# A counter raised by every matmul, and the biases loaded first, in an eight-core attention and FFN layer

## The chip, the cores and the metric

The kernel runs on one Trainium2 chip with all 8 cores. Each core computes 2 of the 16 sequences, with its own copy of the weights; the cores exchange nothing. The time is device microseconds of the slowest core. A core's engines are TensorE (PE in the profile, with its weight loads as PEld), VectorE (DVE), ScalarE (ACT), GpSimd (POOL) and SyncE (SP). Each works through its own list of instructions in order, and they wait for one another by counters (semaphores).

## The reference

`x` has the shape 16 x 4096 x 1024 in f32. There are 16 heads of 64; windows are 256 rows long and advance by 128, and within a window attention is over the 64 x 64 channel pairs of a head, not over rows:

```python
qkv = (x @ W_qkv + b_qkv)                      # 1024 -> 3072
attn = einsum('bhndw,bhnew->bhnde', qw, kw) * 64 ** -0.5
attn = softmax(attn, axis=-1)
o = einsum('bhnde,bhnew->bhndw', attn, vw)     # (b, h, n*d, w) reshaped
x = layernorm(x + o[:, :L] @ W_out + b_out)
gate, up = x @ wg.T, x @ wu.T                  # 1024 -> 3072, int32 weights / 127
x = layernorm(x + (silu(gate) * up) @ wd.T)
```

Since only the first 4096 rows of `o` are kept, 16 windows of each sequence count, made from 17 blocks of 128 rows.

## The kernel before

The program is written by hand, instruction by instruction, engine by engine, inside three blocks. A block ends and the next begins with a barrier of all five engines. Program order is the order in which `build_program` emits, and each instruction that another engine waits for raises a counter by `b.inc`; `b.wait` puts a wait ahead of the next instruction of an engine, unless the engine has waited for that value already. TensorE, VectorE, ScalarE and GpSimd have a counter each ("T", "V", "A", "G"); DMAs have counters of their own and raise them by 16.

The first block (L162 to L220) is the start. POOL clears some tiles and issues 18 DMAs that convert to bf16 on the way: in turns a chunk of 128 rows of `wqkv` (L178) and of `wout` (L180), eight of each, then the biases `bq_bf` and `bo_bf` (L182, L183). All raise "wi0". VectorE waits for all of them and scales the biases by 1/128 (L190, L191). Four rounds spread them over 128 partitions: TensorE multiplies a row of ones with 1024 of the bias elements into PSUM in two matmuls (L206, L207), VectorE copies the result (L214), and the next round waits for that copy. SP waits for the 18 DMAs and the last copy, and so keeps the block open.

The second block is attention and first layernorm, 32 windows on each core. For each block of 128 rows TensorE transposes x (L287), makes q, k and v in three passes (L528 and L533 for the two halves of 1024 columns, 8 chunks each, and L536 and L540 for the bias), and transposes v (L639). For each window it makes the scores of 16 heads in 32 matmuls of 64 columns (L593), transposes the softmax result A in 16 (L671, L673), multiplies it with v in 64 matmuls of 64 columns (L702), and makes the output projection for two blocks of rows (L738, L743, L747, L750). The two heads of a pair write to partitions 0 to 63 and 64 to 127 of PSUM. VectorE copies results out of PSUM, computes the softmax without its exponent and adds the residual; ScalarE evacuates L702's result into `attn_out` (L792), computes the exponent and the layernorm. TensorE also transposes y for the FFN (L322). Between these, the FFN weights are prepared, two jobs per window: POOL loads int32 rows as bf16, VectorE scales them (L403), TensorE transposes them (L417), VectorE copies (L429), POOL writes them to HBM (L439, L442).

The third block is the FFN for 32 groups of 256 rows, with 24 steps each: 8 gate matmuls (L1057) and 8 up matmuls (L1069) of 256 columns, silu on ScalarE (L1156), the product on VectorE (L1092), and 4 down matmuls of 512 columns for the step before (L1036, L1040). The second layernorm runs on ScalarE beside it.

In each group of matmuls one, the last, raises "T", for instance in the gate group:

```python
if dc == 7:
    b.inc(mm, "T", 1)
```

Exceptions are the bias matmuls L206, L207, L536, L540, L747 and L750, each of which raises it. Of the four down matmuls only the last, an L1040, does.

## Time and profile before

| | us |
|---|---|
| three timed runs | 3376.67, 3383.41, 3852.67 |
| their median | 3383.41 |
| profiled execution | 3376.9 |
| its span, slowest core (core 3) | 3375.3 |
| span of the fastest core | 3361.5 |
| PE busy on core 3 | 2936.9 (x23572 matmuls) |
| ACT, DVE, POOL busy | 1247.8, 935.1, 182.9 |

The span is from the first to the last instruction of a core in the profiled execution. Matmuls overlap in the array, and their ends are modelled, so that pace is read from starts: of two neighbours, or of the first and last of a group. A group in the timeline (x8) has one start and the time from there to its last end. "[1.35 <-DVE w_in_bf L403]" behind a row is idle time of that engine before it, and who ended it.

### The profile page before, as it was taken

The numbers are of one execution on the slowest core, as the hardware profiler recorded it, in microseconds if no ns is written. First come the engines' busy times: TensorE is split into PE (matmuls) and PEld (weight loads), VectorE is DVE, ScalarE is ACT, GpSimd is POOL, SyncE is SP. The second block draws the span as 40 slices with busy tenths as digits, with TensorE's granted clock in tenths as the row PEclk, the third lists the DMA queues.
The fourth block names the chain that finished last, engine by engine and source line by source line (L and its number), as shares of the span: only waits on it lengthen the run. The fifth ranks groups of instructions, "written<-read, shape, count | busy, mean of one in ns | idle before, by whom it ended". The sixth has DMA issues, their size and how long they took to land.

```text
span 3375.3 us, 61504 instructions; the slowest of 8 cores (3361.5 to 3375.3 us)
## 1 busy us (share of the span) xinstructions
PE 2936.9 (87%) x23572; PEld 1980.9 (59%) x23572; DVE 935.1 (28%) x1750; ACT 1247.8 (37%) x2721; POOL 182.9 (5%) x324
## 2 busy tenths in 40 slices
PE   1877787788766663999999999999999999999997
PEld 0344444344433332777777777777777777777775
DVE  0444444344434431212212212222212212222221
ACT  0245454525443443223423323323323323323333
POOL 1011111101111100000000000000000000000000
PEclk9999999899988996999999999999999999999998
DMA  7134434333454343411111101101101101111100
GB/s 132 46 99 126 119 108 125 105 87 107 123 130 114 99 155 140 139 38 51 39 38 51 44 33 51 45 32 51 45 32 51 45 33 50 45 38 46 45 32 26
DMA packets 77216, 245.71 MB, mean 73 GB/s; under 512 B 8576, under 2 KB 8576, under 8 KB 76928
## 3 DMA queue, kind: packets, MB, share of 16 engines
q0 software_dynamic: 43744, 138.96, 15.1%
q1 hardware_dynamic: 33184, 102.81, 9.0%
q8 instruction: 193, 3.16, 0.4%
q14 instruction: 95, 0.78, 0.1%
HBM read 175.16 MB, written 102.76 MB: 82 GB/s over the span
## 4 chain that ended last, share of the span: by engine, by line
PE 59%; ACT 0%; DMA 0%; DVE 0%; issue 0%; SPq 0%; POOL 0%; DVEq 0%; ACTq 0%; POOLq 0%
PE psum_qkv L1057 20%; PE psum_O L1036 10%; PE psum_S L1069 10%; PE psum_TR L1069 10%; PE psum_O L1040 10%; DMA wuT<-wuT_scr 0%; DVE y2pre L1116 0%; ACT y L1226 0%; ACT y2sq L1209 0%; ACT y2sq L1206 0%; SPq L1000 0%; ACT L1206 0%; ACT L1156 0%; DVE h_bf L1092 0%; SPq L992 0%
## 5 line engine op out<-in xcount | busy, mean ns | idle before, releaser
L1057 PE MATMUL psum_qkv<-y1fm_sb,wgT 128*128 128x256 bf16 x6144 | 797.9, 273 | 19.5 <-DMA y1fm_sb<-y1fm_scr 19.5
L1057 PEld LDWEIGHTS psum_qkv<-y1fm_sb,wgT 128*128 128x128 bf16 x6144 | 601.8, 98 | 246.8 <-issue 19.7
L1156 ACT ACTIVATE sg_bf<-psum_qkv 128x256 bf16<-128x256 f32 x768 | 293.0, 381 | 1190.6 <-PE psum_qkv L1057 1158.8
L1036 PE MATMUL psum_O<-wdT,h_bf 128*128 128x512 bf16 x1536 | 581.9, 379 | 0.6 <-DVE h_bf L1092 0.6
L1040 PE MATMUL psum_O<-wdT,h_bf 128*128 128x512 bf16 x1536 | 582.0, 379 | 0.0
L1069 PE MATMUL psum_S<-y1fm_sb,wuT 128*128 128x256 bf16 x3072 | 398.9, 273 | 7.7 <-DMA wuT<-wuT_scr 7.7
L1069 PE MATMUL psum_TR<-y1fm_sb,wuT 128*128 128x256 bf16 x3072 | 398.8, 273 | 0.1
L1092 DVE TENSOR_TENSOR h_bf<-psum_TR,sg_bf 128x256 bf16<-128x256 f32 x384 | 163.1, 425 | 795.5 <-PE psum_TR L1069 569.5
L1092 DVE TENSOR_TENSOR h_bf<-psum_S,sg_bf 128x256 bf16<-128x256 f32 x384 | 163.1, 425 | 760.2 <-PE psum_S L1069 756.7
L528 PE MATMUL psum_qkv<-wqkv_bf,x_fm 128*128 128x512 bf16 x816 | 314.4, 385 | 48.3 <-DVE q_tm L561 43.2
L1069 PEld LDWEIGHTS psum_S<-y1fm_sb,wuT 128*128 128x128 bf16 x3072 | 300.8, 98 | 43.2 <-issue 8.1
L1069 PEld LDWEIGHTS psum_TR<-y1fm_sb,wuT 128*128 128x128 bf16 x3072 | 300.9, 98 | 35.6 <-issue 0.3
L533 PE MATMUL psum_qkv<-wqkv_bf,x_fm 128*128 128x512 bf16 x816 | 313.7, 384 | 7.4 <-DVE q_tm L564 6.9
L1036 PEld LDWEIGHTS psum_O<-wdT,h_bf 128*128 128x128 bf16 x1536 | 150.0, 98 | 119.9 <-issue 21.2
L738 PE MATMUL psum_O<-wout_bf,attn_out 128*128 128x512 bf16 x512 | 214.0, 418 | 5.8 <-ACT attn_out L792 5.8
L743 PE MATMUL psum_O<-wout_bf,attn_out 128*128 128x512 bf16 x512 | 210.7, 411 | 0.5 <-ACT attn_out L792 0.5
L1040 PEld LDWEIGHTS psum_O<-wdT,h_bf 128*128 128x128 bf16 x1536 | 150.0, 98 | 98.6
L810 ACT ACTIVATE y1sq<-y1pre 128x1024 f32<-128x1024 f32 x64 | 67.6, 1057 | 305.3 <-DVE y1pre L761 302.1
L528 PEld LDWEIGHTS psum_qkv<-wqkv_bf,x_fm 128*128 128x128 bf16 x816 | 80.4, 98 | 153.6 <-issue 71.1
L533 PEld LDWEIGHTS psum_qkv<-wqkv_bf,x_fm 128*128 128x128 bf16 x816 | 80.6, 99 | 108.8 <-issue 23.4
L1143 POOL DMA_DIRECT2D out<-y x64 | 34.1, 533 | 2019.8 <-ACT y L1190 1860.1
L792 ACT ACT_TABLE_LOAD x32 | 41.1, 1283 | 260.0 <-PE psum_O L702 259.9
(145 smaller groups left out, 2415.5 us busy)
## 6 DMA issues: line engine op xcount, KB each, us to landing
xr<-x SPq DMA_DIRECT2D x64, 512.0 KB, 3.3
y1dbg<-y_f POOLq DMA_DIRECT2D x64, 512.0 KB, 3.0
y1r<-y1dbg SPq DMA_DIRECT2D x64, 512.0 KB, 4.2
out<-y POOLq DMA_DIRECT2D x64, 512.0 KB, 2.9
y1fm_scr<-y1fm_stage POOLq DMA_DIRECT2D x8, 2048.0 KB, 7.7
y1fm_sb<-y1fm_scr SPq DMA_DIRECT2D x32, 512.0 KB, 3.2
xt_bf<-x POOLq DMA_DIRECT2D x34, 256.0 KB, 9.0
wqkv_bf<-wqkv POOLq DMA_DIRECT2D x8, 768.0 KB, 27.2
```

The source lines that it names most:

```text
L528: t_.matmul(psum_qkv[:, 0:512], lhsT, wqkv_bf[:, c, 1024 * p:1024 * p + 512], start=(c == 0), stop=False)
L533: t_.matmul(psum_qkv[:, 512:1024], lhsT, wqkv_bf[:, c, 1024 * p + 512:1024 * (p + 1)], start=(c == 0), stop=False)
L738: t_.matmul(pj[:, 0:512], lhsT, wout_bf[:, c, 0:512], start=(c == 0), stop=False, skip_group_check=True)
L743: t_.matmul(pj[:, 512:1024], lhsT, wout_bf[:, c, 512:1024], start=(c == 0), stop=False, skip_group_check=True)
L792: b.inc(a.activation(attn_out[:, hp, rb:rb + 256] .rearrange("p (d c) -> p d c", c=4), psum_O[:, base:base + 256] .rearrange("p (c d) -> p ...
L810: b.inc(a.activation(y1sq[:, :], y1pre[:, rsl, :], AF.Identity, accum_out=sums[:, rsl, :]), "A", 1)
L1036: t_.matmul(down_ps[:, 1024 * rs:1024 * rs + 512], lhsT, wdT[:, hc, 0:512], start=(hc == 0), stop=(hc == 23), skip_group_check=True)
L1040: mm = t_.matmul(down_ps[:, 1024 * rs + 512:1024 * (rs + 1)], lhsT, wdT[:, hc, 512:1024], start=(hc == 0), stop=(hc == 23), skip_group_che ...
L1057: mm = t_.matmul(gate_ps[hsl], wgT[:, hc, 128 * dc:128 * (dc + 1)], y1fm_sb[:, gsl, dc, :], start=(dc == 0), stop=(dc == 7))
L1069: mm = t_.matmul(up_ps[hsl], wuT[:, hc, 128 * dc:128 * (dc + 1)], y1fm_sb[:, gsl, dc, :], start=(dc == 0), stop=(dc == 7))
L1092: b.inc(v.tensor_tensor(h_bf[:, hsl, :], up_ps[hsl], sg_bf[:, hsl, :], ALU.mult), "V", 1)
L1156: b.inc(a.activation(sg_bf[:, hsl, :], gate_ps[hsl], AF.Silu), "A", 1)
```

## The change

All matmuls and transposes that were silent now raise "T" by one: where the last of a group alone did, each does. The values that other engines wait for grow with it and still mean the group's last. In the first block the two bias DMAs are issued ahead of the weights and have a counter of their own, "wi1"; each chunk of `wqkv` has its own counter ("wv0" to "wv7"); "wi0" is left to `wout`. VectorE's scaling waits for "wi1" alone, SP for all of them. The second block's TensorE no longer waits for "wi0" at its beginning, but for each "wv" counter before the chunk's first matmul in a q, k, v pass and for "wi0" before a projection.

```diff
         @blk.gpsimd
         def _(g):
+            b.inc(g.dma_start(bq_bf[:, :], bqkv_h.ap()), "wi1", 16)
+            b.inc(g.dma_start(bo_bf[:, :], bout_h.ap()), "wi1", 16)
             for c in range(8):
                 b.inc(g.dma_start(wqkv_bf[:, c, :], wqkv_h.ap()[128 * c:128 * (c + 1), :]),
-                      "wi0", 16)
+                      "wv%d" % c, 16)
                 b.inc(g.dma_start(wout_bf[:, c, :], wout_h.ap()[128 * c:128 * (c + 1), :]),
                       "wi0", 16)
-            b.inc(g.dma_start(bq_bf[:, :], bqkv_h.ap()), "wi0", 16)
-            b.inc(g.dma_start(bo_bf[:, :], bout_h.ap()), "wi0", 16)
         wcast_tok = b.tok("wi0")
+        bias_cast_tok = b.tok("wi1")
+        wq_ctok = [("wv%d" % c, 16) for c in range(8)]
         prev_cast = wcast_tok
 
         @blk.vector
         def _(v):
-            b.wait(v, "V", wcast_tok)
+            b.wait(v, "V", bias_cast_tok)
...
         @blk.sync
         def _(q):
             b.wait(q, "Q", prev_cast)
+            b.wait(q, "Q", bias_cast_tok)
+            for tk in wq_ctok:
+                b.wait(q, "Q", tk)
             b.wait(q, "Q", brep_tok)
...
-    a_join_T = [wcast_tok, memset_tok, brep_tok, ("wl0", 16)]
+    a_join_T = [memset_tok, brep_tok, ("wl0", 16)]
...
                         for c in range(8):
+                            b.wait(t_, "T", wq_ctok[c])
                             lhsT = x_fm[:, sl, c, :]
-                            t_.matmul(psum_qkv[:, 0:512],
-                                      lhsT, wqkv_bf[:, c, 1024 * p:1024 * p + 512],
-                                      start=(c == 0), stop=False)
+                            b.inc(t_.matmul(psum_qkv[:, 0:512],
+                                            lhsT, wqkv_bf[:, c, 1024 * p:1024 * p + 512],
+                                            start=(c == 0), stop=False), "T", 1)
...
                                 for par in range(2):
-                                    mm = t_.matmul(
+                                    b.inc(t_.matmul(
                                         psum_O[64 * par:64 * par + 64, dst0:dst0 + 64],
                                         lhsT,
                                         at_bf[:, 128 * hp + 64 * par:128 * hp + 64 * par + 64],
                                         start=True, stop=True,
-                                        skip_group_check=True)
-                                    if hp == 7 and c4 == 3 and par == 1:
-                                        b.inc(mm, "T", 1)
+                                        skip_group_check=True), "T", 1)
...
                         def _(t_, gw=gw, n=n, k2=k2, grt=grt, s=s):
+                            b.wait(t_, "T", wcast_tok)
...
                     for dc in range(8):
-                        mm = t_.matmul(gate_ps[hsl], wgT[:, hc, 128 * dc:128 * (dc + 1)],
-                                       y1fm_sb[:, gsl, dc, :],
-                                       start=(dc == 0), stop=(dc == 7))
-                        if dc == 7:
-                            b.inc(mm, "T", 1)
+                        b.inc(t_.matmul(gate_ps[hsl], wgT[:, hc, 128 * dc:128 * (dc + 1)],
+                                        y1fm_sb[:, gsl, dc, :],
+                                        start=(dc == 0), stop=(dc == 7)), "T", 1)
```

The same edit stands in the groups L287, L322, L417, L533, L593, L639, L671, L673, L738, L743, L1036, L1040 and L1069.

On POOL, at the start, before the change, the biases stand behind the last of the weights:

```order
L178 DMA wqkv_bf<-wqkv 128x3072
L180 DMA wout_bf<-wout 128x1024
L182 DMA bq_bf<-bqkv 1x16x192
L183 DMA bo_bf<-bout 1x16x64
L162 UNCONDITIONAL_BRANCH
L265 UNCONDITIONAL_BRANCH [waits barrier_Pool_Activation_PE_DVE_SP_gather]
```

and after it they stand behind the memsets, ahead of the first weights:

```order
L168 MEMSET a_bd 128x2048
L169 MEMSET lneps 128x1
L176 UNCONDITIONAL_BRANCH
L178 DMA bq_bf<-bqkv 1x16x192
L179 DMA bo_bf<-bout 1x16x64
L181 DMA wqkv_bf<-wqkv 128x3072
L183 DMA wout_bf<-wout 128x1024
```

The two bias DMAs moved past 16 others, and the block's last DMA is now one of `wout`.

On SP, at the end of the first block, before (a counter's name is in the waits, V is VectorE's):

```order
L171 UNCONDITIONAL_BRANCH [waits barrier_Pool_Activation_PE_DVE_SP_release]
L173 DMA ident_sb<-ident 128x128
L217 UNCONDITIONAL_BRANCH
L162 UNCONDITIONAL_BRANCH [waits wi0,V]
L723 UNCONDITIONAL_BRANCH [waits barrier_Pool_Activation_PE_DVE_SP_release]
```

and after:

```order
L172 UNCONDITIONAL_BRANCH [waits barrier_Pool_Activation_PE_DVE_SP_release]
L174 DMA ident_sb<-ident 128x128
L220 UNCONDITIONAL_BRANCH
L163 UNCONDITIONAL_BRANCH [waits wi0,wi1,wv0,wv1,wv2,wv3,wv4,wv5,wv6,wv7,V]
L718 UNCONDITIONAL_BRANCH [waits barrier_Pool_Activation_PE_DVE_SP_release]
```

SP still leaves the block when every weight is there and VectorE has made its last bias copy.

On TensorE, at the start of the second block, after the change (L293 is L287 of before, L529 and L534 are L528 and L533):

```order
L293 MATMUL psum_S<-ident_sb,xt_bf 128x128 [waits xq1]
L293 MATMUL psum_S<-ident_sb,xt_bf 128x128 x7
L521 UNCONDITIONAL_BRANCH
L529 MATMUL psum_qkv<-wqkv_bf,x_fm 128x512 [waits V,wv0]
L534 MATMUL psum_qkv<-wqkv_bf,x_fm 128x512
L529 MATMUL psum_qkv<-wqkv_bf,x_fm 128x512 [waits wv1]
```

Before it these matmuls stand in the same order, and only the first of the pass waits, for V. In the later passes the waits for "wv" are gone, since the engine has waited for those values.

## Rows read from the trace of the kernel before

**Rows 1.** The page: the span, and the busy time of TensorE.

```profile
span 3375.3 us, 61504 instructions; the slowest of 8 cores (3361.5 to 3375.3 us)
...
PE 2936.9 (87%) x23572; PEld 1980.9 (59%) x23572; DVE 935.1 (28%) x1750; ACT 1247.8 (37%) x2721; POOL 182.9 (5%) x324
```

**Rows 2.** Stretches: bounds and length, busy PE, PEld, DVE, ACT, POOL, clock, DMA, GB/s.

```profile
0.00:80.00 80.00, 5.76 (x24) 2.06 (x25) 6.87 (x7) 0.00 (x0) 15.65 (x33) 1.00 0.79 130
...
110.00:1304.00 1194.00, 889.62 (x8039) 467.72 (x8037) 491.40 (x766) 547.75 (x1218) 129.51 (x222) 0.92 0.40 110
1304.00:1340.00 36.00, 6.17 (x32) 4.15 (x33) 3.00 (x5) 1.67 (x2) 2.54 (x3) 0.50 0.57 208
...
1450.00:3375.00 1925.00, 1901.02 (x14505) 1414.61 (x14503) 403.93 (x912) 669.62 (x1436) 33.00 (x62) 0.99 0.11 42
```

**Rows 3.** Timeline, POOL, end of its issues in the first block: start, length, work.

```profile
11.07 0.67 POOL L180 DMA_DIRECT2D wout_bf<-wout  x1
...
12.10 0.64 POOL L183 DMA_DIRECT2D bo_bf<-bout  x1
```

**Rows 4.** Timeline from the bias scaling to the first transpose of x.

```profile
58.66 0.95 DVE L190 TENSOR_SCALAR bq_bf<-bq_bf 1x3072 bf16<-1x3072 bf16 x1 [58.66 <-DMA bo_bf<-bout]
...
60.20 0.58 PE L206 MATMUL psum_qkv<-bq_bf,ones 1*128 1x512 bf16 x1 [60.20 <-DVE bo_bf L191]
...
68.76 1.23 DVE L214 CAST bo_rep<-psum_qkv 128x1024 bf16<-128x1024 f32 x1 [1.26 <-PE psum_qkv L207]
...
70.75 0.57 POOL L268 DMA_DIRECT2D xt_bf<-x  x1 [58.02 <-POOLq L162]
...
76.82 1.01 PE L287 MATMUL psum_TR<-ident_sb,xt_bf 128*128 128x128 bf16 x8 [8.16 <-DMA xt_bf<-x]
```

**Rows 5.** Tile `wout_bf`, its eight transfers: time from issue to landing.

```profile
DMA to landing us min/median/max: 9.0/29.1/45.2
```

**Rows 6.** DMA view of 0 to 80 us: bytes moved, 40 slices of 2 us.

```profile
GB/s 0 16 114 166 154 133 173 145 160 148 169 157 189 166 135 132 174 166 177 194 162 179 168 170 160 170 173 124 41 0 0 0 0 0 0 82 408 206 144 131
```

**Rows 7.** Timeline, TensorE, end of one output projection and start of the next.

```profile
926.73 0.38 PE L743 MATMUL psum_O<-wout_bf,attn_out 128*128 128x512 bf16 x1
926.94 0.38 PE L738 MATMUL psum_O<-wout_bf,attn_out 128*128 128x512 bf16 x1
...
927.38 0.38 PE L747 MATMUL psum_O<-bo_rep,ones 128*128 128x512 bf16 x1
927.59 0.38 PE L750 MATMUL psum_O<-bo_rep,ones 128*128 128x512 bf16 x1
927.81 0.38 PE L738 MATMUL psum_O<-wout_bf,attn_out 128*128 128x512 bf16 x1
```

**Rows 8.** Timeline, TensorE, one step of the FFN.

```profile
2501.02 0.38 PE L1040 MATMUL psum_O<-wdT,h_bf 128*128 128x512 bf16 x1
2501.24 1.04 PE L1057 MATMUL psum_qkv<-y1fm_sb,wgT 128*128 128x256 bf16 x8
2502.11 1.04 PE L1069 MATMUL psum_S<-y1fm_sb,wuT 128*128 128x256 bf16 x8
...
2503.85 1.04 PE L1057 MATMUL psum_qkv<-y1fm_sb,wgT 128*128 128x256 bf16 x8
```

**Rows 9.** Tile `at_bf` in one window: ns min/median/max, first and last start.

```profile
L702 PE MATMUL psum_O<-at_bf,v_fm x64: 189/196/217, 917.0 to 918.0; 128*64 128x64 bf16 x64
```

**Rows 10.** Timeline of the same window: scores, then what follows the V group.

```profile
907.89 0.45 PE L593 MATMUL psum_S<-k_tm,q_tm 128*64 128x64 bf16 x16 [0.73 <-DVE k_tm L561]
...
918.11 0.62 PE L322 MATMUL psum_TR<-ident_sb,y_bf 128*128 128x128 bf16 x8
...
919.55 2.32 ACT L792 ACTIVATE attn_out<-psum_O 128x256 bf16<-128x256 f32 x8
...
921.96 1.01 PE L417 MATMUL psum_qkv<-ident_sb,w_in_bf 128*128 128x128 bf16 x8 [1.35 <-DVE w_in_bf L403]
...
922.77 0.63 PE L738 MATMUL psum_O<-wout_bf,attn_out 128*128 128x512 bf16 x1
```

More of the change, by code:

```diff
@@ L286, in _ @@
                 for c in range(8):
[L287 to L291 removed]
+                    b.inc(t_.transpose(tr_slice(bi, 128 * c, 128 * (c + 1)),
+                                       xt_bf[:, xsl, 128 * c:128 * (c + 1)],
+                                       ident_sb[:, :]), "T", 1)
             tx_done[gt2] = b.tok("T")
@@ L701, in _ @@
                                 for par in range(2):
-                                    mm = t_.matmul(
+                                    b.inc(t_.matmul(
                                         psum_O[64 * par:64 * par + 64, dst0:dst0 + 64],
@@ L1035, in _ @@
                         lhsT = h_bf[:, hsl, 128 * rs:128 * (rs + 1)]
-                        t_.matmul(down_ps[:, 1024 * rs:1024 * rs + 512],
-                                  lhsT, wdT[:, hc, 0:512],
-                                  start=(hc == 0), stop=(hc == 23),
-                                  skip_group_check=True)
-                        mm = t_.matmul(down_ps[:, 1024 * rs + 512:1024 * (rs + 1)],
-                                       lhsT, wdT[:, hc, 512:1024],
-                                       start=(hc == 0), stop=(hc == 23),
-                                       skip_group_check=True)
-                        if rs == 1:
-                            b.inc(mm, "T", 1)
+                        b.inc(t_.matmul(down_ps[:, 1024 * rs:1024 * rs + 512],
+                                        lhsT, wdT[:, hc, 0:512],
+                                        start=(hc == 0), stop=(hc == 23),
+                                        skip_group_check=True), "T", 1)
+                        b.inc(t_.matmul(down_ps[:, 1024 * rs + 512:1024 * (rs + 1)],
+                                        lhsT, wdT[:, hc, 512:1024],
+                                        start=(hc == 0), stop=(hc == 23),
+                                        skip_group_check=True), "T", 1)
                 down_done[(g, hc)] = b.tok("T")
@@ L1068, in _ @@
                     for dc in range(8):
-                        mm = t_.matmul(up_ps[hsl], wuT[:, hc, 128 * dc:128 * (dc + 1)],
-                                       y1fm_sb[:, gsl, dc, :],
-                                       start=(dc == 0), stop=(dc == 7))
-                        if dc == 7:
-                            b.inc(mm, "T", 1)
+                        b.inc(t_.matmul(up_ps[hsl], wuT[:, hc, 128 * dc:128 * (dc + 1)],
+                                        y1fm_sb[:, gsl, dc, :],
+                                        start=(dc == 0), stop=(dc == 7)), "T", 1)
                 up_done[(g, hc)] = b.tok("T")
```

68 lines of the change are left out of this document (27 added, 41 removed), and 2 rows, old and new, of the table b.

## The prediction

> **What bounds the kernel now.** I read the page's shares first, then the table of stretches, then the timelines of the start, of one attention window and of one FFN step. TensorE is busy 87% of the span [rows 1], a mean over stages. The stretches part them: TensorE is busy 5.8 of the first 80 us, 890 of 1194 between 110 and 1304, and 1901 of 1925 after 1450 [rows 2]. So there are three stages with three limits: a start of some 80 us that waits for weights, an attention stage of some 1220 us in which TensorE, VectorE and ScalarE hand work to one another, and an FFN stage of some 2050 us in which only TensorE's pace counts. The change touches TensorE in all three, and the order of the start.
>
> **The start: the biases move to the head of the POOL queue.** Now: the last of 16 weight transfers is issued at 11.07 us, the last of two bias transfers behind them at 12.10 [rows 3]. VectorE waits for all 18 and begins scaling at 58.66, when the bias issued last lands. Two scalings and four rounds of two bias matmuls and a cast follow, the rounds from 60.20 to 68.76 + 1.23 = 69.99. Only then is the block closed: POOL issues its first x load at 70.75, after 58 us without work, and TensorE transposes x at 76.82 [rows 4].
> After: scaling and rounds wait for the biases alone, which come first, and run under the weight transfer: 69.99 - 58.66 = 11.3 us of work against some 50 of transfer. The block ends with the last weight. When is that? The slowest weight transfer took 45.2 us [rows 5]; taken for the last issue, 11.07 + 45.2 = 56.3. The bytes agree: of slices of 2 us the one from 54 to 56 still moves 124 GB/s, the one from 56 to 58 only 41, the next none [rows 6]. Two bias issues ahead of the weights cost 12.10 - 11.07 = 1.0 us of POOL's time, so the last weight lands at about 57.3. Saved: 69.99 - 57.3 = 12.7 us. From below, if the weights end only where the last bias now does: 11.3. From above, if the bias issues cost nothing in front: 69.99 - 56.3 = 13.7. I take 12.7; the 0.8 us to POOL's issue and the 6.1 us from there to the first transpose stay behind it, and the x load is what is late next.
> The new waits: SP waits on eleven counters in place of two, all reached when the weights are there; cost 0. TensorE gets a wait for a weight chunk ahead of eight matmuls of the first pass, and one at the first projection. All of TensorE's work is queued behind each, but SP has waited for every chunk before this block opens, so they are met. The nearest row is the output projection's L738 at 926.94, which has a ScalarE wait that is met: it starts 0.21 us after the matmul before it [rows 7], no later than one without a wait. I take 0; at most 9 x 0.2 = 1.8 us, if each cost a matmul's step.
>
> **The signal on every matmul.** Before, a group of 8 to 64 matmuls raises the counter at its last alone; after, nearly each of the 23572 does. The consumers still wait for the group's last count, so no wait moves; what can change is TensorE's pace, or when the last count arrives.
> Wide matmuls. The trace has signalling ones. L747 and L750 both signal: they start at 927.38 and 927.59, the next, a silent one, at 927.81, the same 0.21 to 0.22 us as between silent ones [rows 7]. In the FFN L1040 at 2501.02 signals and the gate group starts 0.22 us later; one of the eight gate matmuls signals, and the up group starts after 0.87 us, eight steps of 0.109 with nothing over [rows 8]. So the FFN step (2.61 us from gate to gate [rows 8], 768 times, 2004 us) stays. I take 0 for the 20000 matmuls of 128 columns and more; that rows are read to 0.01 us leaves a bound of 0.005 us each, which is a rival below. A gain is excluded: nothing is removed.
> Narrow matmuls. Here no row has consecutive signals. The 64 V matmuls of a window start between 917.0 and 918.0, 16 ns apart [rows 9]; the 32 score matmuls come in two groups of 16 in 0.45 us, with one's own 0.2 taken off 17 ns apart [rows 10]. Such steps are possible because two matmuls that write the two halves of the partitions overlap. What follows is on the path: behind the V group TensorE goes to the transposes L322, then waits 1.35 us for VectorE's scaling L403, and the projection L738 starts at 922.77, when L417 is through. ScalarE's leg is the shorter one: its copies end at 919.55 + 2.32 = 921.87, 0.9 us before L738 [rows 10]. So a later V group makes a later window, nearly one for one.
> The price from below is 0. From above, with the overlap of a pair gone, a 64-column matmul takes half of a 128-column one, which stand (0.62 - 0.2) / 7 = 60 ns apart in L322 [rows 10], so 30 ns; the 16 A transposes, paired and of 128 columns, lose at most as much each: 64 x 14 + 32 x 13 + 16 x 30 = 896 + 416 + 480 ns, 1.8 us a window, 57 us in 32 windows. The row nearest in kind is the signal on two neighbours [rows 7], at no cost; I take 0, with less trust than for the wide ones.
> The rows say only that signals 0.2 us apart are free. The Trainium skill speaks against the change for narrow ones: "TensorE: Matmul & The Clock Gate", section "The cost: per-tile semaphore tail", has the increments of matmuls that share the array go out one after another, about 26.3 ns each. By it, as an estimate, a window would be longer by 64 x (26.3 - 16) + 32 x (26.3 - 17) ns, 0.96 us, and 32 windows by 31 us; the sum would be 3395. It would leave the wide ones alone. No run so far shows it.
>
> **Sum.** The profiled execution took 3376.9 us, its span 3375.3, with 14 us between the spans of its cores [rows 1]; the three timed runs took 3376.67, 3383.41 and 3852.67, so it stands 6.5 us under their median. Sum: 3376.9 - 12.7 + 0 + 0 = 3364.2. Against the median it would be 3370.7; I give 3370.
>
> **Rivals.**
> A, signals go out one at a time. In the score and V groups of the attention stage the next matmul, or the last count, is held to a step longer than 16 ns. For it: these steps are thirteen times denser than any row with neighbouring signals. Against it: no row. It turns the result to slower than before once it costs more than 12.7 us / (32 x 96) = 4.1 ns per narrow matmul. At half the upper bound the time is 3370 + 28 = 3398, at the full one 3427. If only the last count is late and TensorE is not held, the L322 behind it catches up part: half again, 3384.
> B, the gain at the start is taken back later. The end of the attention stage could hang on transfers that don't shift: there TensorE is busy 6 of 36 us [rows 2]. Against it: the last weight writes follow VectorE's copies, which follow the same TensorE queue, and so shift with it. Time 3383, as before.
> C, every matmul is dearer. At 2 ns each, under what the rows resolve, 23572 x 2 ns = 47 us: 3417; at 5 ns, 3488. Against it: 0.109 and 0.217 leave no visible room between signalling and silent ones.
> D, the change does less than it says: the bias scaling doesn't run early, since the biases land late though issued first. Against it: they are small, and what now delays them is the queue ahead. Time as in B.
>
> **Chances.** Forecast (start gained, signals free or nearly) 0.52; A 0.30; B and D 0.10; C 0.08. The range reaches down to the fastest timed run less the gain's upper bound, 3376.67 - 13.7 = 3363, and some us of spread between cores below it; up to A at half its bound and as much spread above: 3358 to 3405. It leaves out A at its full price and most of C. 2% of the time, about what a measurement of this kernel tells from no change, is 68 us: faster by that has no mechanism (0.01), slower needs C above 3.4 ns, or A and C together (0.05), within 2% 0.94.
>
> **What would show it.** In the changed kernel's timeline the bias scaling begins before 15 us and POOL's first x load is at about 58; the V group again spans 1.0 us; a score group's consumer on VectorE starts as soon behind it; an FFN step is 2.61 us. If the V group spans 1.7 us, or ScalarE starts later behind it, A holds. If the FFN step is longer by 0.03 us, C does. A first x load later than 61 us refutes the start's part.

## Result and profile after

The changed kernel takes 3415.78 us in the median. Set against the kernel before on the same chip, the ratio is 1.012 with a 95% interval of 1.0073 to 1.0168: slower by some 41 us, though by less than 2%. The profiled execution took 3412.78 against 3376.9. The forecast was 3370, its range ended at 3405. In some executions, whatever the kernel, some cores show a lower granted clock and take longer (from e5 on in most, where the kernel before took 3377 to 3427), so that times here leave such executions or such cores out, and small differences are best read from ratios and from cores at the same clock.

The page after, against [rows 1]:

```profile
span 3411.2 us, 61521 instructions; the slowest of 8 cores (3397.3 to 3411.2 us)
...
PE 2970.8 (87%) x23572; PEld 1996.2 (59%) x23572; DVE 935.3 (27%) x1750; ACT 1248.5 (37%) x2721; POOL 183.1 (5%) x324
```

VectorE, ScalarE and GpSimd do the same work in the same time; only TensorE's busy time grew, by 34 us with the same number of matmuls. So some matmuls became longer. Where? The gate group's line has its first and last start in both traces. Before, then after:

```profile
L1057 PE MATMUL psum_qkv<-y1fm_sb,wgT x6144: 272/273/421, 1327.2 to 3348.7; 128*128 128x256 bf16 x199
```

```profile
L1051 PE MATMUL psum_qkv<-y1fm_sb,wgT x6144: 272/273/417, 1363.8 to 3384.6; 128*128 128x256 bf16 x199
```

The FFN stage takes 2021.5 us before and 2020.8 after, although all of its 15,360 matmuls (768 steps of 20) now signal. It only begins 36.6 us later. The start, against [rows 4]:

```profile
5.67 0.97 DVE L193 TENSOR_SCALAR bq_bf<-bq_bf 1x3072 bf16<-1x3072 bf16 x1 [5.67 <-DMA bo_bf<-bout]
...
15.80 1.23 DVE L217 CAST bo_rep<-psum_qkv 128x1024 bf16<-128x1024 f32 x1 [1.26 <-PE psum_qkv L210]
60.31 1.59 POOL L274 DMA_DIRECT2D xt_bf<-x  x3 [47.21 <-POOLq L163]
...
69.33 1.01 PE L293 MATMUL psum_TR<-ident_sb,xt_bf 128*128 128x128 bf16 x8 [53.63 <-DMA xt_bf<-x]
```

The biases are scaled at 5.67 and spread by 17 us, under the weight transfer. POOL's first x load goes out at 60.31 in place of 70.75, and TensorE transposes x at 69.33 in place of 76.82: 7.5 us earlier. Core 3 gained less than most: over the eight cores the first transpose of x starts at 78.2 us in the mean before and at 67.8 after, 10.4 us earlier. On core 3, from there to the first gate matmul is the attention stage: 1327.2 - 76.8 = 1250.4 us before, 1363.8 - 69.3 = 1294.5 after. It lost 44.1 us in 32 windows, and that is the whole loss.

One window of it, in the timeline after (start, length, engine, line):

```profile
906.15 1.49 PE L699 MATMUL psum_O<-at_bf,v_fm 128*64 128x64 bf16 x64 [1.32 <-DVE at_bf L681]
...
907.57 0.62 PE L326 MATMUL psum_TR<-ident_sb,y_bf 128*128 128x128 bf16 x8
908.57 1.28 ACT L788 ACT_TABLE_LOAD   x1 [7.42 <-PE psum_TR L326]
908.87 0.69 DVE L340 COPY y1fm_stage<-psum_TR 128x1024 bf16<-128x1024 bf16 x1 [2.87 <-PE psum_TR L326]
...
910.04 0.61 PE L419 MATMUL psum_S<-ident_sb,w_in_bf 128*128 128x128 bf16 x8 [1.85 <-DVE w_in_bf L405]
...
912.80 0.63 PE L734 MATMUL psum_O<-wout_bf,attn_out 128*128 128x512 bf16 x1
```

and before, the window of [rows 9, 10]:

```profile
916.97 1.20 PE L702 MATMUL psum_O<-at_bf,v_fm 128*64 128x64 bf16 x64 [1.32 <-DVE at_bf L684]
...
918.25 1.28 ACT L792 ACT_TABLE_LOAD   x1 [7.91 <-PE psum_O L702]
918.83 0.69 DVE L338 COPY y1fm_stage<-psum_TR 128x1024 bf16<-128x1024 bf16 x1 [2.01 <-PE psum_TR L322]
...
920.00 0.61 PE L417 MATMUL psum_S<-ident_sb,w_in_bf 128*128 128x128 bf16 x8 [1.28 <-DVE w_in_bf L403]
```

Count from the first V matmul. TensorE leaves the group after 1.42 us in place of 1.14. ScalarE, which waits for the group's last count, starts its table load after 2.42 in place of 1.28. VectorE, which waits for the last of the eight L326 transposes behind the group, copies after 2.72 in place of 1.86. From VectorE's copy hangs the chain over the scaling, the transposes L419 and the projection L734, which starts after 6.65 in place of 5.80 (922.77 in [rows 10]). TensorE's wait ahead of the first L419 group grows from 1.28 to 1.85 us; that and the 0.28 us in the V group make the 0.85. The count comes later than the work: TensorE began L326 at 907.57, one microsecond before ScalarE heard that the group ahead of it was over.

A second thing changed, the clock. In the stretches view, in the columns of [rows 2] (the granted clock is the third value from the end), from the end of the V group to the projection and then the projection's beginning, before and after:

```profile
918.00:922.70 4.70, 2.08 (x35) 1.75 (x29) 2.05 (x4) 4.11 (x10) 0.56 (x1) 0.89 0.29 55
922.80:925.00 2.20, 2.20 (x8) 0.80 (x7) 0.57 (x1) 0.00 (x0) 0.00 (x0) 0.50 0.29 119
```

```profile
907.50:912.70 5.20, 2.01 (x29) 1.68 (x26) 2.05 (x4) 4.11 (x10) 0.56 (x1) 0.80 0.52 93
912.80:917.20 4.40, 4.40 (x13) 1.60 (x12) 0.69 (x1) 0.00 (x0) 0.55 (x1) 0.50 0.16 65
```

TensorE runs at 0.50 (1.2 GHz) over the first 2.2 us of the projection before and over 4.4 us after, and at 1.00 (2.4 GHz) behind it. The fall comes earlier, among the waits and the weight transposes: the means of 0.89 and 0.80 hold 1.0 us at 0.50 before and 2.1 us after. So the slow stretch was already in the trace of before, at the place that [rows 10] show: the L738 at 922.77 lasts 0.63 us where those of [rows 7] last 0.38. The means of the two groups of projection matmuls, over the whole run, before and after:

```profile
L738 PE MATMUL psum_O<-wout_bf,attn_out 128*128 128x512 bf16 x512 | 214.0, 418 | 5.8 <-ACT attn_out L792 5.8
```

```profile
L734 PE MATMUL psum_O<-wout_bf,attn_out 128*128 128x512 bf16 x512 | 227.7, 445 | 8.4 <-ACT attn_out L788 8.4
```

A projection matmul lasts 0.38 us at the full clock and 0.63 at half of it, so the mean tells the share at half the clock. The other group, L743, goes from 411 to 437 ns. On average 26.5 ns more: 26.5 / 250 of 1024 matmuls, some 108, fell to half the clock, and each then steps by 0.43 us in place of 0.22. That is 23 us. Counted in the traces of core 3, 143 of the 1024 last longer than 0.5 us before and 252 after. The direct delay is 0.85 us in the 28 windows that have weight transposes, 24 us. Together 47, against 44 measured.

### The profile page after: what moved, and what is told of

Read it like the earlier page. It is cut to its first block, busy times and chain, and to the rows that moved or that the text cites. A ratio compares the mean times of both kernels' runs of the same rounds, so it can differ in the third digit from the quotient of the medians.

```text
span 3411.2 us, 61521 instructions; the slowest of 8 cores (3397.3 to 3411.2 us)
## 1 busy us (share of the span) xinstructions
PE 2970.8 (87%) x23572; PEld 1996.2 (59%) x23572; DVE 935.3 (27%) x1750; ACT 1248.5 (37%) x2721; POOL 183.1 (5%) x324
## 4 chain that ended last, share of the span: by engine, by line
PE 59%; ACT 0%; DMA 0%; DVE 0%; issue 0%; SPq 0%; POOL 0%; ACTq 0%; DVEq 0%; POOLq 0%
PE psum_qkv L1051 20%; PE psum_O L1032 10%; PE psum_S L1061 10%; PE psum_TR L1061 10%; PE psum_O L1036 10%; DMA wuT<-wuT_scr 0%; DVE y2pre L1106 0%; ACT y L1216 0%; ACT y2sq L1199 0%; ACT y2sq L1196 0%; SPq L996 0%; ACT L1196 0%; SPq L988 0%; DVE h_bf L1082 0%; ACT l2ln L1212 0%
## 5 line engine op out<-in xcount | busy, mean ns | idle before, releaser
L1036 PE MATMUL psum_O<-wdT,h_bf 128*128 128x512 bf16 x1536 | 582.2, 379 | 0.0
L529 PE MATMUL psum_qkv<-wqkv_bf,x_fm 128*128 128x512 bf16 x816 | 315.5, 387 | 48.9 <-DVE q_tm L562 44.3
L534 PE MATMUL psum_qkv<-wqkv_bf,x_fm 128*128 128x512 bf16 x816 | 314.6, 386 | 7.6 <-DVE q_tm L565 7.1
L734 PE MATMUL psum_O<-wout_bf,attn_out 128*128 128x512 bf16 x512 | 227.7, 445 | 8.4 <-ACT attn_out L788 8.4
L739 PE MATMUL psum_O<-wout_bf,attn_out 128*128 128x512 bf16 x512 | 224.0, 437 | 0.4 <-ACT attn_out L788 0.4
L1036 PEld LDWEIGHTS psum_O<-wdT,h_bf 128*128 128x128 bf16 x1536 | 150.1, 98 | 99.0 <-issue 0.3
L529 PEld LDWEIGHTS psum_qkv<-wqkv_bf,x_fm 128*128 128x128 bf16 x816 | 80.6, 99 | 155.0 <-issue 73.1
L534 PEld LDWEIGHTS psum_qkv<-wqkv_bf,x_fm 128*128 128x128 bf16 x816 | 80.9, 99 | 109.2 <-issue 24.2
```

What stands on the lines that cost most here:

```text
L529: b.inc(t_.matmul(psum_qkv[:, 0:512], lhsT, wqkv_bf[:, c, 1024 * p:1024 * p + 512], start=(c == 0), stop=False), "T", 1)
L534: b.inc(t_.matmul(psum_qkv[:, 512:1024], lhsT, wqkv_bf[:, c, 1024 * p + 512:1024 * (p + 1)], start=(c == 0), stop=False), "T", 1)
L734: b.inc(t_.matmul(pj[:, 0:512], lhsT, wout_bf[:, c, 0:512], start=(c == 0), stop=False, skip_group_check=True), "T", 1)
L739: b.inc(t_.matmul(pj[:, 512:1024], lhsT, wout_bf[:, c, 512:1024], start=(c == 0), stop=False, skip_group_check=True), "T", 1)
L1036: b.inc(t_.matmul(down_ps[:, 1024 * rs + 512:1024 * (rs + 1)], lhsT, wdT[:, hc, 512:1024], start=(hc == 0), stop=(hc == 23), skip_group_ch ...
```

## Experiments

Each kernel is the kernel before with some hunks of the change, or e1 or the changed kernel with one more edit. The totals of e3 to e8 are of one execution each; the starts of ScalarE and VectorE within a window, though, are the same on all eight cores, in the median over the windows of each. A signal is a count raised by a matmul. The groups' lines shift by a few: L709 or L715 is the V group, L328 or L331 the y transposes, L344 or L347 VectorE's copy of them, L744 to L752 the projection.

**e1: the start alone.** All hunks of the start, with the weight counters and the waits on them; the groups signal once, as before.

> Only the start of the change: biases first, own counters, the new waits; signals as before. All theories: TensorE's first transpose of x at about 69.3 us as in the changed kernel (76.8 before), the attention stage and the FFN as before. So a profiled execution of about 3376.9 - 7.5 = 3369 us. If it stays at 3377, the gain at the start is taken back later by itself; if it is above 3385, the start edit is part of the loss.

Median 3369.93; ratio 0.9974 (0.9963 to 0.9985), 8.8 us faster. Core 3:

```profile
59.74 1.59 POOL L274 DMA_DIRECT2D xt_bf<-x  x3 [46.63 <-POOLq L163]
...
65.48 1.01 PE L293 MATMUL psum_TR<-ident_sb,xt_bf 128*128 128x128 bf16 x8 [49.78 <-DMA xt_bf<-x]
```

The mean first transpose of x over the eight cores is at 68.6 us, 9.6 earlier than before. The reordering does what was forecast, and the new waits cost nothing visible. The loss lies in the signals.

**e2: the signals alone.** All signal hunks, the start as before.

> Only the signals of the change: every matmul raises T, the start as before. If the two edits add up, the profiled execution is 3376.9 + 44 = 3421 us (the changed kernel's 3412.8 plus the 7.5 us of the start). The V group again takes 1.49 us from start to last end and ScalarE starts 2.4 us behind its first matmul. Rival: the start shift itself moved the clock's dips, then the signals alone cost less than 36 us and this comes out under 3413.

Three times from 3421.19 to 3427.03; ratio 1.0133 (1.011 to 1.0156), so 45 us slower. Start and signals add up to the change: -8.8 + 45 = 36, measured 41 with an interval that holds it.

**e3: wide signals.** The changed kernel with the narrow groups (scores, A transposes, V) back to one signal each:

```diff
-                                    b.inc(t_.matmul(
+                                    mm = t_.matmul(
                                         psum_O[64 * par:64 * par + 64, dst0:dst0 + 64],
...
-                                        skip_group_check=True), "T", 1)
+                                        skip_group_check=True)
+                                    if hp == 7 and c4 == 3 and par == 1:
+                                        b.inc(mm, "T", 1)
```

> The changed kernel, with only the score, A-transpose and V groups (the narrow matmuls) silent but for their last. Theory Q (signals leave TensorE one by one, some 34 ns each, so only groups denser than that queue up): all of the 44 us go, time about 3369 us, ScalarE starts 1.3 us behind the first V matmul. Rival C (every signal costs TensorE something): 20000 signals are left, so most of the 44 us stay, 3400 us or more.

3368.8 us, against 3370.3 of e1's profiled run. Some 20,000 signals by matmuls of 128 to 512 columns, 56 ns and more apart, cost nothing that shows in one execution; rival C falls.

**e4: the V group's signals alone**, on top of e1:

```diff
-                                    mm = t_.matmul(
+                                    b.inc(t_.matmul(
                                         psum_O[64 * par:64 * par + 64, dst0:dst0 + 64],
...
-                                        skip_group_check=True)
-                                    if hp == 7 and c4 == 3 and par == 1:
-                                        b.inc(mm, "T", 1)
+                                        skip_group_check=True), "T", 1)
```

> The start edit and signals on each of the 64 V matmuls of a window, all other groups silent but for their last. Theory Q: the V group's last count is late by 64 x (34 - 16) = 1.15 us, VectorE and TensorE behind it by less; most of the loss is here: 3369 + 30 to 40 = 3400 to 3410 us. If the score group or the transposes carry as much, it stays under 3390.

3408.83 us, 38.5 above e1. Its window, core 5, where the V group starts at 901.56:

```profile
903.98 1.28 ACT L798 ACT_TABLE_LOAD   x1 [7.03 <-PE psum_TR L328]
904.10 0.69 DVE L344 COPY y1fm_stage<-psum_TR 128x1024 bf16<-128x1024 bf16 x1 [2.69 <-PE psum_TR L328]
...
908.03 0.63 PE L744 MATMUL psum_O<-wout_bf,attn_out 128*128 128x512 bf16 x1
```

ScalarE after 2.42 us as in the full change, VectorE after 2.54, the projection after 6.47. This group alone brings nearly the whole loss. The difference to the full change, 0.18 us at VectorE, fits the seven more signals of L326, which queue behind the 64 (7 x 25 ns, worked out below). The kernel ran once more under the label e10 (nothing in it is reordered, despite the label):

> The same kernel as e4 (start edit, signals on all 64 V matmuls), timed in rounds: its one time was 3408.8 us. Theory Q with the V group as sole cause: the ratio to the kernel before equals that of the whole change, 1.012 within 0.003.

Ratio 1.0076 (1.0043 to 1.0109) to before, some 26 us, and with e1's 9 us, 35 from these signals: the same, more roughly. It is below the 1.012 within 0.003 that was expected, though the intervals overlap; what e4 lacks to the full change, 4 us, is part of that.

**e6 and e8: half and three quarters of the 64 signals.** e6 has `if par == 1:` ahead of the signal (32), e8 `if par == 1 or c4 % 2 == 0:` (48).

> Start edit; one matmul of each pair in the V group signals: 32 signals, one per 33 ns of TensorE's pace. Theory Q with 34 ns a signal: 32 x 34 = 1.09 us against 1.03 us for the group, so it is free within 0.1 us a window: 3369 to 3372 us. If instead a signal ends the overlap of its pair, it costs as much as all 64: 3400 us or more.

> Start edit; 48 of the 64 V matmuls signal. Theory Q alone, in proportion to the delay of the last count: 48 x 34 - 1030 = 0.6 us against 1.15 us, so about half of the 39 us: 3388 us. With the clock in it (theory K: the wait behind the group makes the stretch at 1.2 GHz in the output projection longer, 8 cold matmuls a window in place of 5): the time need not be in proportion; if the granted clock of the cores is still 0.963 to 0.965, the time is 3369 + 0.45 x 32 = 3383 or less, if it has fallen to 0.957, 3395 or more.

e6's cores 0 to 5 took 3359.3 to 3370.4, e1's cores 3354.6 to 3368.8. Its core 3:

```profile
906.60 1.20 PE L709 MATMUL psum_O<-at_bf,v_fm 128*64 128x64 bf16 x64 [1.32 <-DVE at_bf L691]
...
908.22 1.28 ACT L800 ACT_TABLE_LOAD   x1 [8.23 <-PE psum_O L709]
908.46 0.69 DVE L344 COPY y1fm_stage<-psum_TR 128x1024 bf16<-128x1024 bf16 x1 [2.01 <-PE psum_TR L328]
...
912.40 0.63 PE L746 MATMUL psum_O<-wout_bf,attn_out 128*128 128x512 bf16 x1
```

e8 took 3388.53, 18 us over e1. Its core 3:

```profile
886.68 1.28 PE L709 MATMUL psum_O<-at_bf,v_fm 128*64 128x64 bf16 x64 [1.32 <-DVE at_bf L691]
...
888.69 1.28 ACT L800 ACT_TABLE_LOAD   x1 [6.89 <-PE psum_TR L328]
888.81 0.69 DVE L344 COPY y1fm_stage<-psum_TR 128x1024 bf16<-128x1024 bf16 x1 [2.27 <-PE psum_TR L328]
...
892.74 0.63 PE L746 MATMUL psum_O<-wout_bf,attn_out 128*128 128x512 bf16 x1
```

| signals of 64 | ScalarE after | VectorE after | projection after | profiled run against e1 |
|---|---|---|---|---|
| 1 (before) | 1.28 | 1.86 | 5.80 | |
| 32 (e6) | 1.62 | 1.86 | 5.80 | 0 to +4 (cores 0 to 5) |
| 48 (e8) | 2.01 | 2.13 | 6.06 | +18 |
| 64 (e4) | 2.42 | 2.54 | 6.47 | +38.5 |

From 32 to 48 to 64, ScalarE's start moves by 0.39 and 0.41 us, 25 ns for each matmul that signals where it was silent. At 64 all are signalling: with the 0.25 us that ScalarE takes after the last of a group (before: 1.28 less the 1.03 over which the group starts), (2.42 - 0.25) / 64 = 34 ns each. So a silent one takes 34 - 25 = 9 ns. The law that fits all three: a group's matmuls leave a queue one after another, a signalling one in 34 ns, a silent one in 9. Since the 25 ns are the slope between these runs, e6 is a weak check (32 x 34 + 32 x 9 = 1.38, + 0.25 = 1.63, measured 1.62). A better one is VectorE's start, which waits for the eight transposes behind the V group. In e4 and e8 seven of these are silent and one signals, 7 x 9 + 34 = 0.10 us behind ScalarE's start (measured 0.12 and 0.12); in the changed kernel all eight signal, 8 x 34 = 0.27 (measured 0.30). Before, the matmuls start 16 ns apart and silent ones leave faster than that, so nothing piles up.

The table also says which consumer counts. In e6 ScalarE is 0.34 us late and the projection starts no later: its leg had 0.9 us of slack, as worked out from [rows 10]. Only VectorE's delay reaches the projection, one for one (0.27 to 0.26, 0.68 to 0.67). And each total is about twice its direct part: e8 28 x 0.26 = 7 of 18, e4 28 x 0.67 = 19 of 38.5.

**e5: the same 64 signals to a counter that nobody waits for.** The last one alone raises "T":

```diff
                                     if hp == 7 and c4 == 3 and par == 1:
                                         b.inc(mm, "T", 1)
+                                    else:
+                                        b.inc(mm, "D", 1)
```

> Start edit; 63 of the 64 V matmuls of a window raise a counter D that nobody waits for, the last raises T as before. If signals leave TensorE through one path, whatever the counter (theory Q), ScalarE still starts 2.4 us behind the first V matmul and the time is that of all 64 on T, about 3408 us. If the queue belongs to the counter T, it is free: 3369 us.

Cores 2 to 7 took 3387 to 3402 (e4's cores 3387 to 3407), core 3 3402.2. There:

```profile
902.30 1.49 PE L709 MATMUL psum_O<-at_bf,v_fm 128*64 128x64 bf16 x64 [1.32 <-DVE at_bf L691]
...
904.73 1.28 ACT L802 ACT_TABLE_LOAD   x1 [8.75 <-PE psum_TR L328]
```

2.43 us, as in e4. The queue is one of the engine and not one of the counter.

**e7: the score groups' signals alone**, with the same edit at L600.

> Start edit; the 32 score matmuls of a window all signal, the V group only with its last. Theory Q: two bursts of 16, each 16 x (34 - 17) = 0.27 us late at its end; VectorE's maximum starts 0.27 us later, but TensorE goes on with the third pass and VectorE has slack there: 3369 to 3373 us. If TensorE itself is held, 0.5 us x 32 = 17 us: 3386 us.

3366.89 us, no loss. Second score group and its consumer, core 4 of e7, then core 3 before:

```profile
897.31 0.45 PE L600 MATMUL psum_S<-k_tm,q_tm 128*64 128x64 bf16 x16
...
898.19 0.69 DVE L612 TENSOR_REDUCE negmax<-psum_S 128x8 f32<-128x512 f32 x1 [1.02 <-PE psum_S L600]
```

```profile
942.63 0.45 PE L593 MATMUL psum_S<-k_tm,q_tm 128*64 128x64 bf16 x16 [0.15 <-DVE k_tm L564]
...
943.25 0.69 DVE L607 TENSOR_REDUCE negmax<-psum_S 128x8 f32<-128x512 f32 x1 [0.77 <-PE psum_S L593]
```

VectorE starts 0.88 us behind the group in place of 0.62. The law says 16 x (34 - 17) = 0.27, 17 ns being their own step [rows 10], and 0.26 it is. But the run is no longer, so the delay is hidden there: the mechanism acts on this dense group too, and costs only where the consumer is on the path.

**e11: work for TensorE while it waits.** e1, with four matmuls of 512 columns ahead of each group of weight transposes, into the bank that the transposes then overwrite:

```diff
-                    b.wait(t_, "T", dq_tok)
                     b.wait(t_, "T", tr_free)
                     b.wait(t_, "T", qtok)
+                    for _f in range(4):
+                        t_.matmul(tr_bank(bi), ones128[:, :], bq_rep[:, 0:512],
+                                  start=True, stop=True, skip_group_check=True)
+                    b.wait(t_, "T", dq_tok)
```

> The start edit with signals as before, and four matmuls of 512 columns whose result is overwritten put ahead of each group of weight transposes, where TensorE has 1.3 us of waiting for VectorE's scaling and the bank is free: work that fills a wait, 0.86 us each, two per window. Theory K (those waits are what the stretch at 1.2 GHz at each output projection comes from): fewer cold projection matmuls (mean of L738/L743 under 395 ns in place of 410), granted clock above 0.975, time 3369 - 10 to 15 = about 3357 us. Rival: the clock does not answer to this filler, or the filler delays the transposes: 3369 us or more.

3342.38 us in its profiled run, ratio 0.9868 (0.9817 to 0.992). Core 1:

```profile
889.36 1.20 PE L715 MATMUL psum_O<-at_bf,v_fm 128*64 128x64 bf16 x64 [1.32 <-DVE at_bf L697]
...
892.83 1.03 PE L425 MATMUL psum_qkv<-bq_rep,ones 128*128 128x512 bf16 x4
...
894.34 0.61 PE L429 MATMUL psum_qkv<-ident_sb,w_in_bf 128*128 128x128 bf16 x8 [0.48 <-DVE w_in_bf L412]
...
894.78 0.38 PE L752 MATMUL psum_O<-wout_bf,attn_out 128*128 128x512 bf16 x1
```

```profile
894.80:898.00 3.20, 3.20 (x18) 1.45 (x16) 0.00 (x0) 0.00 (x0) 0.18 (x1) 1.00 0.23 87
```

```profile
L752 PE MATMUL psum_O<-wout_bf,attn_out 128*128 128x512 bf16 x512 | 195.4, 382 | 5.8 <-ACT attn_out L806 5.8
```

TensorE does more, eight matmuls a window whose result nobody reads, and the run is 28 us faster than e1: the clock is 1.00 through the projection, its matmuls last 382 ns in the mean, and the last transposes run at full pace too, so that the projection starts 5.42 us behind the V group in place of 5.80. The gain had been forecast at 12, and is over twice that. Its parts make more than the whole: 0.38 x 28 = 11 us for the earlier start, and 28 / 250 of 1024 projection matmuls at 0.21 us, 24 us. Where the other 7 us go is not shown.

The Trainium skill, "TensorE: Matmul & The Clock Gate", section "Why this matters for your kernels", advises against idle gaps between bursts of matmuls, since the clock then falls to its lower level. The traces agree that it falls, but each wait is shorter here than the gaps that the page warns of: those of 1.28 and 1.35 us ahead of the two L417 groups are followed by a projection at 0.50, and the filled ones, with 0.48 us left ahead of the second, by 1.00.

**e12: the V group's signals with the filler**, both edits on e1. It parts the direct delay from the clock.

> As e4 (start edit, signals on all 64 V matmuls), with the same filler. If the loss of 39 us is the late count alone (0.85 us x 32 = 27 us) plus the clock's part of some 12 to 17, and the filler takes the cold stretch away, then this stands 27 us above e11, with the same mean of the projection's matmuls as e11: about 3384 us. If the loss has no clock part, it stands 39 us above e11.

Ratio 0.9926 (0.9892 to 0.996); profiled 3360.54, so 18 us over e11. Core 1:

```profile
871.06 1.49 PE L715 MATMUL psum_O<-at_bf,v_fm 128*64 128x64 bf16 x64 [1.32 <-DVE at_bf L697]
...
877.17 0.38 PE L750 MATMUL psum_O<-wout_bf,attn_out 128*128 128x512 bf16 x1
```

The projection starts 6.11 us behind the V group against e11's 5.42: 0.69 x 28 = 19. With the clock held up, the late count costs its direct part and nothing more. Without the filler it was 38.5, so 20 us of e4's loss came by the clock. The expectation had 27 us, from 0.85 us in 32 windows: the full change's delay in place of this group's, and four windows too many.

**e9: may the first block end early?** e1, with the three first x loads ahead of the weights, all of `wqkv` ahead of `wout`, and SP not waiting for any weight:

```diff
             b.inc(g.dma_start(bo_bf[:, :], bout_h.ap()), "wi1", 16)
+            for gt2 in range(3):
+                b.inc(g.dma_start(xt_bf[:, gt2, :], x_h.ap()[0, 128 * gt2:128 * (gt2 + 1), :]),
+                      "xq%d" % gt2, 16)
...
         def _(q):
-            b.wait(q, "Q", prev_cast)
             b.wait(q, "Q", bias_cast_tok)
-            for tk in wq_ctok:
-                b.wait(q, "Q", tk)
             b.wait(q, "Q", brep_tok)
```

> A version that should beat both: signals as before, biases first, then the first three x blocks, then all of wqkv, then wout; the first block no longer waits for the weights, each q, k, v pass waits chunk by chunk. Theory (the start is bound by the weights' transfer, and then needlessly by x behind it): the first pass ends when the last wqkv chunk lands, at about 5 + 12/16 x 52 = 44 us, where in e1 it ended at 77 us; 33 us earlier at that place, 25 to 33 us at the end: 3336 to 3344 us. Rival: the first projection then waits for wout and the FFN weight rows queue behind it, or the start shift is lost to the clock: less than 12 us gained on e1, 3357 us or more.

A miss: 3361.79 and 3362.89, only 8 us under e1. In the timeline of core 3:

```profile
66.19 1.05 POOL L397 DMA_DIRECT2D w_in_bf<-wg  x2 [51.51 <-POOLq L163]
66.19 1.01 PE L294 MATMUL psum_TR<-ident_sb,xt_bf 128*128 128x128 bf16 x8 [50.50 <-PEq L163]
```

No instruction of the first block waits for a weight any more, and x has landed; still both engines leave the block (L163 is its end) at 66. The instructions of the block's end on core 3 say why:

```profile
L163 POOLq DRAIN  x1: 55241/55241/55241, 10.3 to 10.3; - x1
```

POOL's part of the block's end is a DRAIN, in its own queue behind its DMA issues; here it lasts 55.2 us, to 65.5. The bytes moved, slice by slice of 2 us:

```profile
GB/s 0 16 4 100 165 163 143 154 132 178 154 166 172 157 175 151 172 169 172 178 154 178 181 154 161 169 187 153 169 164 172 45 1 0 274 254 131 147 169 187
```

The traffic, longer by the x loads in it, ends in the slice from 62 to 64, the last of `wout` lands at 64.6, and the DRAIN ends 0.9 us later. So the end of the block itself waits for the transfers that POOL issued, and e13 takes it away. The same DRAIN ends at 59.3 us in the kernel before, where the bias casts last longer, and at 59.6 in the changed kernel, 0.7 us ahead of POOL's first x load at 60.31.

**e13: no end between the blocks.** As e9, with the first two blocks made one, so that TensorE waits for its own chunk alone (SP's waits at the end of the first block go, and ScalarE gets one for POOL's memsets).

> The start's term: first and second block joined into one, so no barrier and no drain of POOL's transfers stands between them; biases, three x blocks, wqkv, wout in this order. In e9 POOL left the first block only at 65.8 us, when its own transfers were through, though nothing in the program waited for them. Theory D (the end of a block drains POOL's transfers): now the first pass ends with the last wqkv chunk at about 45 us instead of 77 in e1; time 3369 - 32 = 3337 us, or 3345 if the first window then waits for wout and the FFN weight rows. If something else held the first pass, 3360 us as e9.

Ratio 0.9926 (0.9871 to 0.9982). Core 3 took 3337.0 against 3354.7 in e1. The end of its first pass:

```profile
52.37 0.58 PE L537 MATMUL psum_qkv<-wqkv_bf,x_fm 128*128 128x512 bf16 x1 [4.10 <-DMA wqkv_bf<-wqkv]
...
53.60 0.63 PE L549 MATMUL psum_qkv<-bq_rep,ones 128*128 128x512 bf16 x1
```

x is transposed at 21.1, each chunk of `wqkv` is used as it lands, some 4.7 us apart, and the pass is over at 53.6; in e1 that was at 73.6. The 20 us reach the end nearly whole: 17.7 on this core, 16 by the ratios, with 14 us between the cores of e1. The forecast was 32 us, with the first pass at 45, and missed by half: its last chunk lands later, and e1's first pass had ended at 73.6 and not at 77. So the counters per chunk, which in the changed kernel are met before anyone looks at them, are worth something once the barrier is gone.

**e14: both** (e13 and the filler), and **e15**, the changed kernel with the filler.

> e13 with the filler of e11. The two gains lie in different stages and should add: 3369 - 32 - 27 = 3310 us, between 3305 and 3325.

> The whole changed kernel with the filler of e11. By the split found so far (late signals 18 us, clock 21 us of the V group's 39) the whole change with the filler stands 18 to 23 us above e11's 3342 us: 3360 to 3365 us, the projection's matmuls at a mean of 380 to 390 ns. If the other groups' signals (scores, transposes, wide ones) cost something that the clock had hidden, it is above 3370.

e14: ratio 0.9796 (0.9686 to 0.9906), its fastest execution 3325.8, its core 0 at 3305.6 us. It is the fastest of all and beats both kernels; the forecast was 3305 to 3325. e15: ratio 0.9943 (0.9898 to 0.9988), cores 0 to 3 at 3348.5 to 3361.7, the slowest of them in the forecast's 3360 to 3365. The filler turns the change's loss into a gain, but with one signal per group it is worth more (e11, 0.9868).

## Why the prediction was wrong

**What bounds the kernel: right.** Three stages with three limits; the FFN hung on TensorE's pace alone and did not move.

**The start, -12.7: right in kind, too large.** The biases were scaled at 5.67 us (foreseen: before 15). The first transpose of x came 7.5 us earlier on core 3 and 10.4 in the mean of the cores (9.6 in e1); by e1's ratio the start gave 8.8. Two terms were off. The block closed later than the last weight's landing was taken to be: POOL's load at 60.31, foreseen at 58.1. The last weight was issued at 12.46, 1.4 us later than before where 1.0 was worked out, and took 46.4 us in place of 45.2, so it landed at 58.9, foreseen at 57.3. The bytes per slice after the change agree:

```profile
GB/s 0 16 20 117 157 149 134 171 130 157 164 172 163 199 169 131 166 166 157 171 200 161 179 178 161 166 170 167 122 5 70 342 114 176 171 138 140 164 195 64
```

The slice from 56 to 58 still moves 122 where it moved 41 before [rows 6]. From that landing to POOL's load it is 1.4 us more, through the DRAIN of e9, where the sum had 0.8. And the x load took 69.33 - 60.31 = 9.0 us in place of 6.1, which the sum had kept fixed; over the cores of the three runs it takes 5.6 to 10.5, and the 6.1 was one of the short ones. The lower bound of 11.3 was no bound, since it left out both.

**The new waits, 0: right.** e1 has them all and loses nothing.

**Wide signals, 0: right.** The reading of neighbouring starts, signalling and silent, at 0.21 and 0.109 us [rows 7, 8] held for 20,000 matmuls (e3). One exception is small: the seven signals of L326 that stand behind the V group, 0.18 us at VectorE.

**Narrow signals, 0: the step that failed.** It was this: "The row nearest in kind is the signal on two neighbours [rows 7], at no cost; I take 0". Those neighbours are 210 ns apart, and a queue that needs 34 ns per entry never shows behind them. The V matmuls are 16 ns apart, the row was not near at all. What a price of zero at a wide spacing bounds is the price of one signal, up to that spacing, and the place at which to expect it is where the spacing is smallest. The prediction did name that place and chose against it. What the runs showed in its place is 34 ns for each signal, 1.14 us at the group's last count and 0.85 us at the projection, 24 us in 28 windows. The prediction's own sign for it, ScalarE starting later behind the group, was met.

**Rival A was the truth**, but not in its working. Its forms were two: TensorE held to the longer step, or only the last count late. Both happened: TensorE by 0.28 us per window, ScalarE's count by 1.14. Its upper price, from the overlap of a pair, was 30 ns per V matmul; 34 was measured, so it was no upper bound for this group. Its places were three; only V reached the end. The scores' 0.26 us are hidden (e7), and e4 leaves little for the A transposes. It had the path right, from the V group over the L322 transposes to VectorE, with ScalarE's leg 0.9 us shorter. But it took the transposes to catch up half of a late count once TensorE itself is free. They catch up only 0.28 of 1.14 us, since their own counts stand behind the V group's in the queue.

The Trainium skill, "TensorE: Matmul & The Clock Gate", section "The cost: per-tile semaphore tail", has for a pack of small matmuls 25 ns, 4.7 for each matmul and 26.3 more for each increment. The runs agree in form and nearly in size: 9 for each matmul and 25 more for a signal. The prediction had used the increment's term alone and set it against the step of 16 ns; with both terms, as an estimate by that page, 31 ns each make 0.96 us of lateness in the V group, where 1.14 was measured.

**What no term held: the clock.** Half of the loss (20 of e4's 38.5, by e12 and e11) came from a stretch at 1.2 GHz at the projections, which was there before and went from 2.2 to 4.4 us of the projection when the wait ahead grew from 1.28 to 1.85. The row was in the prediction's own group: a projection matmul of 0.63 us in [rows 10] beside 0.38 in [rows 7], and it was passed over. That a longer wait lengthens the slow stretch is seen in e8 and e4, and with the filler (e12) it does not; why, and by how much for a given wait, stays open. Each microsecond of direct delay brought about as much again here, or somewhat more (18 us for 7 in e8).

**Rivals B, C, D.** The start's gain was not taken back (e1), wide matmuls were not dearer (e3), the reordering did what it says.

**The range.** On the forecast's basis the start gave 2 to 4 us less and the attention stage took 44 us more: 3370 + 2 to 4 + 44 = 3416 to 3418, against 3415.78. Without the clock's part, some 20 us, this would have ended inside the range. The prediction's estimate of 3395 is set on the profiled execution; on the forecast's 3370, as the other rivals are, it would be 3401, inside the range too. The range ended at half of A's upper price, and left its full price, 3427, out; With the densest steps of the kernel named in A and such a price at hand, 0.30 was too low for it.

## What to carry to other kernels

Let only the last matmul of a group signal, above all where matmuls start closer than some 34 ns (64-column pairs at 16 ns here); signals at 56 ns and more apart cost nothing here, unless a denser group stands ahead of them, so that they can be kept there if they are of use. When a count comes late, look at every group that stands behind it on the engine, and ask which consumer has slack. Where TensorE waits between bursts on the critical path, look at the lengths of the first matmuls behind the wait; if they are at half the clock, work that nobody needs, put into the wait, can pay (28 us here), and a count that comes later there can cost about twice its delay.

## What the runs showed of the hardware that was not expected

- A matmul that raises a counter takes 34 ns in a queue of TensorE, a silent one 9, as worked out from e4, e6 and e8. The queue holds the counts of later groups, whatever counter they raise (e5), and when it is long it holds TensorE itself: the V group is left after 1.42 us in place of 1.14.
- TensorE's clock was at 0.50 for the first 2.2 us of an output projection of the kernel before, behind waits of 1.28 and 1.35 us with eight transposes between them; 143 of the 1024 projection matmuls of core 3 were slow. Four matmuls of 512 columns in each wait kept it at 1.00 (e11).
- The end of a block kept the engines until POOL's transfers had landed, though none of the program's waits was for them: POOL's DRAIN lasted to 65.5 us and the engines went on at 66.19 in e9. With the blocks joined (e13) the first pass was over at 53.6.
